# Score products of both head halves issued as one piece, in the four quarters of TensorE's array

## The chip, the cores and the metric

One core of one Trainium2 chip runs the kernel. The metric is the time of one execution on the device, in microseconds (us). The runs of the kernel before are given as a median of three; one further execution was profiled, and every row below comes from it.

## The reference, cut to what matters

128 images of 64x64 pixels and 128 channels go through a tower: a depthwise 3x3 convolution with 8x8 average pooling makes 64 tokens per image; then come a single-head attention, a mixture of ten experts (two shared, eight routed with the top two chosen), a second attention with eight heads, and a last two-layer block over channels. The change touches the scores of the second attention. Per image and head they are

```python
comp_scores = jnp.einsum('bhqd,bhkd->bhqk', q, k_c) / scale
comp_scores = jnp.where(causal_c[None, None], comp_scores, -jnp.inf)
win_scores = jnp.einsum('bhqd,bhkd->bhqk', q, k) / scale
win_scores = jnp.where(win_mask[None, None], win_scores, -jnp.inf)
all_scores = jnp.concatenate([comp_scores.astype(f32), win_scores.astype(f32), sink.astype(f32)], axis=-1)
attn = jax.nn.softmax(all_scores, axis=-1).astype(x.dtype)
```

With 64 tokens there are 64 window keys, 15 compressed keys (together LK = 79) and one sink column, so 80 scores per query and head. The head dimension is 16.

## The kernel before, in words

The images are worked on in 16 groups of eight (512 tokens, four tiles of 128 tokens, two images per tile). Four stages lie one iteration apart: while group g is tokenised (tok), group g-1 is in its first attention (att), g-2 in the experts (ffn) and g-3 in the second attention and last block (sec); 19 iterations in all. In the text "group n" is the n-th group (from 0) whose second attention is in the stretch looked at.

The order of work is written out by hand. ORDER (from line 57) holds one list of pieces per engine for one iteration, and each engine works through its own list strictly in order; semaphores make the pieces wait for each other. Nothing is planned at run time. The names of the pieces that matter here:

- score (PE line 637, DVE line 1271): the scores of one tile and one half of the heads. There are eight per group, n = 0 to 7, tile n // 2, half n % 2. TensorE first writes the mask and sink of 4 heads x 80 columns into the half's own PSUM bank (L647: place_b times limit_b, bf16, all 128 output partitions), and then adds two products (L651, fp32, 316 columns), one per image of the tile. A product contracts over the 64 partitions of the half (rows 0 to 63 or 64 to 127 of the array) and has 64 output partitions (columns 0 to 63 or 64 to 127). Each fp32 product stands in the trace as two matmul records, its two passes. From n = 2 on the mask waits until VectorE has read piece n - 2, that is the last piece in the same bank.
- VectorE reads a score piece with a maximum (L1275) and a subtraction into e3 (L1277), in its own list's order, with other work between some pieces.
- exp (ACT, L904): two exponentials of 1280 columns, behind pieces 3 and 7. In ScalarE's list the piece stands ahead of narrow.5's copy.
- turn and value (L662, L671): the transposes of e3 and the products with the values. turn.0 needs both exponentials. They use the same two banks, sec_bank[0] and sec_bank[1].
- post.0 and post.1 (L418, L681): the output projection; VectorE adds its result at L1293, and the last block follows.
- lift, widen, narrow (L566, L581 to L583, L593 and L597): the routed experts' blocks, 15 per group. widen.7 uses the bank of narrow.5, so it waits until ScalarE has copied narrow.5's result.
- pool.u.k (L446, L450, L456): pooling products. pool.1.3 waits for VectorE's inner.1.1 (L1064), which stands behind score.1 in VectorE's list. att.7 and att.8 (L418, L489) are the transposes and products of the first attention.

Each of these has its own wait, for example for the score pieces

```python
if n >= 2:
    eng.wait_ge(s3_step, at(s3_step, g, 2 * (n - 2) + 2))
```

where s3_step counts two steps of VectorE per piece.

Of the kernel before, what the change touches and what calls it, by code (L numbers as in the profile page):

```python
# [19 lines left out]
NI, HW, C = 128, 64, 128  # L20
P = 128
BX = 8
L = BX * BX
# [11 lines left out]
LK = L + LC  # L35
LCP = 16
HH = HEADS // 2
# [25 lines left out]
        up.0 up.1 table up.2 down.0 up.3 down.1 down.2 up.4 up.5 out' up.6 down.3 down.4 up.7 down.5 down.6  # L63
        down.7 lift.0 pool.0.0 pool.0.1 widen.0 lift.1 widen.1 att.1 lift.2 narrow.0 lift.3 pool.0.2 att.2 lift.4
        widen.2 att.3 pre.2 narrow.1 pre.3 pool.0.3 widen.3 pre.4 att.4 pre.6 lift.5 narrow.2 pool.1.0 pool.1.1
        lift.6 narrow.3 pre.5 widen.4 pre.7 pool.1.2 widen.5 score.0 lift.7 score.1 score.2 pool.1.3 narrow.4
        score.3 lift.8 score.4 score.5 att.7 score.6 score.7 narrow.5 widen.6 att.8 turn.0 widen.7 pool.2.0
        lift.9 pool.2.1 turn.1 value.0 narrow.6 lift.10 turn.2 pool.2.2 value.1 widen.8 turn.3 pool.2.3 value.2
        narrow.7 turn.4 value.3 lift.11 att.10 turn.5 value.4 widen.9 att.11 value.5 turn.6 narrow.8 turn.7
        value.6 widen.10 att.12 lift.12 value.7 narrow.9 narrow.10 lift.13 post.0 widen.11 post.1 widen.12  # L70
        lift.14 narrow.11 pool.3.0 widen.13 narrow.12 pool.3.1 widen.14 narrow.13 pool.3.2 post.3 narrow.14
        pool.3.3 post.4 post.5""",
    act="""
        hidden.0 table hidden.1 hidden.2 hidden.3 hidden.4 hidden.5 out' hidden.6 hidden.7 lift.0 pool.0.0 lift.1
        widen.0 lift.2 att.1 narrow.0 lift.3 widen.1 att.2 pre.2 narrow.1 att.3 lift.4 gate widen.2 pool.0.2
# [16 lines left out]
    pool="""  # L92
# [23 lines left out]
def program(nc, x, conv_w, conv_b, wq, bq, wk, bk, gate_w, gate_b, w1, b1, w2, bias, sb2,  # L116
            swq, swqs, swk, swks, swv, swkc, swvc, swo, comp_gate, sink, tw1, tb1, tw2, tb2,
            ident_c, block_c, cos_c, sin_c, mask1_c, limit_c, place_c, part_c, heads_c, before_c, route_c, out):
    with ExitStack() as ctx:
# [16 lines left out]
        def at(s, g, k):  # L136

            return g * per[id(s)] + k
# [275 lines left out]
        def _(eng):  # L414
# [186 lines left out]
            def layer2(g, b, kind, n=0):  # L601
# [21 lines left out]
                elif kind == "pre" and n in (6, 7):  # L623
                    if n == 6:
                        eng.wait_ge(rope_read, at(rope_read, g, 4))
                        for t in range(T):
                            mm = nc.tensor.matmul(b1[:, t * C:(t + 1) * C], x3t[:, t * P:(t + 1) * P], second["v"][:],
                                                  start=True, stop=True)
                    else:
                        eng.wait_ge(xc_step, at(xc_step, g, 8))  # L630
                        eng.wait_ge(kc_ready, at(kc_ready, g, 1))
                        for k in range(2):
                            mm = nc.tensor.matmul(b0[:, k * C:(k + 1) * C],
                                                  xc[:, 4 * k:4 * k + 4, :].rearrange("p i w -> p (i w)"), second["vc"][:],
                                                  start=True, stop=True)
                    mm.then_inc(v_done, 1)
                elif kind == "score":
                    t, half = n // 2, n % 2
                    bank = sec_bank[half]
                    if n == 0:  # L640
                        eng.wait_ge(keys_ready, at(keys_ready, g, 1))
                        eng.wait_ge(kc_ready, at(kc_ready, g, 1))
                        eng.wait_ge(v_ready, at(v_ready, g, 2))
                    if n >= 2:
                        eng.wait_ge(s3_step, at(s3_step, g, 2 * (n - 2) + 2))
                    wide, rows = bank[:, 0:HH * (LK + 1)], slice(half * C // 2, (half + 1) * C // 2)
                    nc.tensor.matmul(wide, place_b[:], limit_b[:, half].rearrange("p h k -> p (h k)"),  # L647
                                     start=True, stop=False)
                    for im in range(2):
                        tok = (2 * t + im) * L  # L650
                        mm = nc.tensor.matmul(  # L651
                            wide[im * L:(im + 1) * L].rearrange("p (h k) -> p h k", h=HH)[:, :, 0:LK],
                            q3[rows, tok:tok + L], keys_h[rows, :, 2 * t + im, :],
                            start=False, stop=True)
                    mm.then_inc(scored, 1)
                elif kind == "turn":
                    if n == 0:
                        eng.wait_ge(e3_ready, at(e3_ready, g, 2))
                    if n >= 1:
                        eng.wait_ge(p3t_ready, at(p3t_ready, g, n))  # L660
                    for h in range(HH):
                        mm = nc.tensor.transpose(b0[0:LK + 1, h * P:(h + 1) * P], e3[:, n, h, :], ident[:])  # L662
                    mm.then_inc(p3_turned, 1)
                elif kind == "value":
                    t, half = n // 2, n % 2
                    eng.wait_ge(p3t_ready, at(p3t_ready, g, n + 1))
                    if n >= 1:
                        eng.wait_ge(o3_ready, at(o3_ready, g, n))
                    for h in range(HH):
                        for im in range(2):  # L670
                            mm = nc.tensor.matmul(b1[im * L:(im + 1) * L, h * (HD + 1):(h + 1) * (HD + 1)],  # L671
                                                  p3t[:, half, h, im * L:(im + 1) * L],
                                                  values[:, 2 * t + im, half * HH + h, :], start=True, stop=True)
                    mm.then_inc(o3_done, 1)
                elif kind == "post" and n == 0:
                    eng.wait_ge(o3_ready, at(o3_ready, g, 8))
                    turn_tiles(b0, lambda t: o3[:, t, :], ident[:]).then_inc(o3_turned, 1)
                elif kind == "post" and n == 1:
                    eng.wait_ge(o3t_ready, at(o3t_ready, g, 1))
                    for t in range(T):  # L680
                        mm = nc.tensor.matmul(b1[:, t * P:(t + 1) * P], o3t[:, t * P:(t + 1) * P], second["o"][:],  # L681
                                              start=True, stop=True)
                    mm.then_inc(wo_done, 1)
                elif kind == "post" and n == 3:
                    eng.wait_ge(x4_ready, at(x4_ready, g, 4))
                    turn_tiles(b0, lambda t: x3[:, t, :], ident[:]).then_inc(x4_turned, 1)
                elif kind == "post" and n == 4:
                    eng.wait_ge(x4t_ready, at(x4t_ready, g, 1))
                    nc.tensor.matmul(b1[:], tw1_s[:], x3t[:], start=True, stop=True).then_inc(up_done, 1)
                elif kind == "post" and n == 5:  # L690
                    eng.wait_ge(up_ready, at(up_ready, g, 1))
                    for t in range(T):
                        mm = nc.tensor.matmul(b0[:, t * P:(t + 1) * P], o3t[:, t * P:(t + 1) * P], tw2_s[:],
                                              start=True, stop=True)
                    mm.then_inc(mlp_done, 1)
# [797 lines left out]
```

## Time and profile before

| | us |
|---|---|
| runs of the kernel before, median of 3 | 1969.28 |
| lowest and highest of them | 1950.7 and 1969.51 |
| the profiled execution's own time | 1981.56 |
| span of the profiled execution (first to last instruction) | 1979.8 |
| TensorE busy in it | 1588.2 |
| VectorE busy in it | 1417.9 |
| mean granted clock of TensorE | 0.866 |

The span is what the views of the trace cover; the time of the execution lies 1.8 us above it. A granted clock of 1.00 is 2.4 GHz, 0.50 is 1.2 GHz, and a value between them is a mean over a stretch that has both. Start times count from the start of the span. PE is TensorE, DVE is VectorE, ACT is ScalarE and POOL is GpSimd.

### The profile page before, as it was taken

The numbers are of one execution on the slowest core, as the hardware profiler recorded it, in microseconds if no ns is written. First come the engines' busy times: TensorE is split into PE (matmuls) and PEld (weight loads), VectorE is DVE, ScalarE is ACT, GpSimd is POOL, SyncE is SP. The second block draws the span as 40 slices with busy tenths as digits, with TensorE's granted clock in tenths as the row PEclk, the third lists the DMA queues.
The fourth block names the chain that finished last, engine by engine and source line by source line (L and its number), as shares of the span: only waits on it lengthen the run. The fifth ranks groups of instructions, "written<-read, shape, count | busy, mean of one in ns | idle before, by whom it ended". The sixth has DMA issues, their size and how long they took to land.

```text
span 1979.8 us, 42922 instructions
## 1 busy us (share of the span) xinstructions
PE 1588.2 (80%) x14896; PEld 1190.4 (60%) x14896; DVE 1417.9 (72%) x3372; ACT 1002.2 (51%) x2581; POOL 797.3 (40%) x643
## 2 busy tenths in 40 slices
PE   0132878989898988989898989898898989998846
PEld 0021665757666675767576676667676766666623
DVE  3767677878877787888778788778887787642322
ACT  0112546555555646565555547365656555564622
POOL 2335363544526263545436263625444352504020
PEclk9975888998879797998889789879989897979965
DMA  7556564453735544554536455445546364202000
GB/s 295 216 192 230 195 221 181 162 208 145 260 134 193 211 170 163 196 202 155 211 143 227 172 188 220 143 178 201 205 141 231 140 240 156 62 7 62 13 22 6
DMA packets 109125, 331.56 MB, mean 167 GB/s; under 512 B 13662, under 2 KB 87585, under 8 KB 92412
## 3 DMA queue, kind: packets, MB, share of 16 engines
q1 hardware_dynamic: 86416, 300.90, 41.3%
q0 software_dynamic: 8992, 19.42, 2.9%
q10 hardware_dynamic: 13516, 8.50, 1.4%
q8 instruction: 133, 2.18, 0.5%
q14 instruction: 68, 0.56, 0.1%
HBM read 299.48 MB, written 29.29 MB: 166 GB/s over the span
## 4 chain that ended last, share of the span: by engine, by line
PE 43%; DVE 18%; POOL 15%; issue 11%; DMA 6%; ACT 5%; ACTq 2%; SPq 0%; POOLq 0%; DVEq 0%
PE hid_bank L597 10%; PE sec_bank L651 5%; POOL yg L1375 5%; POOL xbuf L1364 4%; DMA xbuf<-in_x 4%; PE hid_bank L582 3%; PE sec_bank L671 3%; PE sec_bank L662 3%; PE hid_bank L581 3%; DVE xbuf L1064 3%; DVE xbuf L1060 3%; POOL rows_d L1353 2%; DVE xc L1269 2%; POOL rs L1336 2%; PE hid_bank L583 2%
## 5 line engine op out<-in xcount | busy, mean ns | idle before, releaser
L1364 POOL TENSOR_TENSOR xbuf<-xbuf 128x512 f32<-128x512 f32 x256 | 343.3, 1341 | 587.3 <-DVE xbuf L1060 578.7
L597 PE MATMUL hid_bank<-w_s,hid 128*128 x1920 | 329.5, 324 | 0.0
L842 ACT ACTIVATE hid<-hid_bank,bias_t 128x128 f32<-128x128 f32 x960 | 272.1, 377 | 83.2 <-PE hid_bank L583 78.9
L597 PEld LDWEIGHTS hid_bank<-w_s,hid 128*128 128x128 f32 x1920 | 278.4, 223 | 18.7
L581 PE MATMUL hid_bank<-xt,w_b 128*128 128x128 bf16 x960 | 221.1, 239 | 57.8 <-ACT ys L852 30.3
L1060 DVE TENSOR_TENSOR xbuf<-xbuf 128x1536 f32<-128x1536 f32 x128 | 224.3, 1752 | 19.8 <-DMA xbuf<-in_x 19.8
L1353 POOL DMA_INDIRECT rows_d<-x2r,spot_i x128 | 159.5, 1246 | 195.8 <-DVE owned L1211 163.4
L582 PE MATMUL hid_bank<-xt,w_b 128*128 128x128 bf16 x960 | 222.2, 240 | 0.4
L583 PE MATMUL hid_bank<-xt,w_b 128*128 128x128 bf16 x960 | 218.4, 236 | 0.0
L1085 DVE SCALAR_TENSOR_TENSOR taps<-pooled_s,tapw,taps 128x256 f32<-128x256 f32 (+1 forms) x416 | 208.6, 501 | 8.3
L1068 DVE TENSOR_TENSOR xbuf<-xbuf 128x1024 bf16<-128x1024 f32 x128 | 173.5, 1355 | 24.2 <-DMA xbuf<-in_x 24.2
L833 ACT ACTIVATE xt<-down_bank 128x256 bf16<-128x256 bf16 x240 | 93.2, 388 | 185.6 <-PE down_bank L566 185.5
L1375 POOL DMA_INDIRECT yg<-outs_d,spot_i x128 | 145.4, 1136 | 54.0 <-issue 39.5
L581 PEld LDWEIGHTS hid_bank<-xt,w_b 128*128 x960 | 98.8, 103 | 86.7 <-issue 78.4
L825 ACT ACTIVATE hid<-hid_bank,b_s 128x512 f32<-128x512 f32 x128 | 87.3, 687 | 120.8 <-PE hid_bank L530 98.2
L769 ACT ACTIVATE pooled_s<-pool_bank 128x384 f32<-128x384 f32 x192 | 95.0, 497 | 89.2 <-PE pool_bank L450 70.9
L1275 DVE TENSOR_REDUCE m<-sec_bank 128x4 f32<-128x320 f32 x128 | 62.7, 490 | 106.0 <-PE sec_bank L651 105.4
L1064 DVE TENSOR_TENSOR xbuf<-xbuf 128x512 bf16<-128x512 f32 x128 | 107.5, 840 | 43.2 <-POOL xbuf L1364 43.1
L446 PE MATMUL pool_bank<-block_b,xbuf 128*128 128x48 bf16 x1024 | 49.7, 190 | 106.7 <-DVE xbuf L1064 62.7
L909 ACT ACTIVATE p3t<-sec_bank 80x512 f32<-80x512 f32 x128 | 76.3, 596 | 116.3 <-PE sec_bank L662 116.3
L542 PEld LDWEIGHTS down_bank<-w_s,hid 128*128 128x128 f32 x1024 | 129.1, 198 | 10.1 <-issue 1.1
L1336 POOL TENSOR_TENSOR rs<-ve,power 128x4 f32<-128x4 f32 x64 | 83.9, 1310 | 124.6 <-DVE ve L1045 123.0
(216 smaller groups left out, 3344.2 us busy)
## 6 DMA issues: line engine op xcount, KB each, us to landing
xbuf<-in_x SPq DMA_DIRECT2D x128, 2048.0 KB
rows_s<-rows_d SPq DMA_DIRECT2D x48, 320.0 KB, 8.1
outs_d<-ys SPq DMA_DIRECT2D x240, 64.0 KB, 1.8
out<-h ACTq DMA_DIRECT2D x16, 256.0 KB
w_s<-in_w ACTq DMA_DIRECT2D x1, 2560.0 KB
hid<-in_w POOLq DMA_DIRECT2D x10, 256.0 KB, 3.4
rows_d<-x2r,spot_i POOLq DMA_INDIRECT x128
yg<-outs_d,spot_i POOLq DMA_INDIRECT x128
```

The costliest lines, as they stand in the source:

```text
L581: nc.tensor.matmul(out_q, w_high, high, start=True, stop=False)
L582: nc.tensor.matmul(out_q, w_low, high, start=False, stop=False)
L583: mm = nc.tensor.matmul(out_q, w_high, low, start=False, stop=True)
L597: mm = nc.tensor.matmul(hid_bank[n % 2][:, 0:P], hid[:, n % RING, q * P:(q + 1) * P], w_q, start=False, stop=q == FC - 1)
L842: ins = nc.scalar.activation(hid[:, n % RING, cols], hid_bank[n % 2][:, cols], ACT.Gelu, bias=bias_t[:, q, j:j + 1])
L1060: nc.vector.tensor_tensor(v[:, :, 1:6:2, :], v[:, :, 1:6:2, :], v[:, :, 2:7:2, :], ALU.add) \
L1064: nc.vector.tensor_tensor(halves[k][:, :, 1, 0, :], blocks[k][:, :, 1, :], halves[k][:, :, 1, 1, :], ALU.subtract).then_inc(inner_low, 1)
L1068: nc.vector.tensor_tensor(halves[k][:, :, 0:8:7, 0, :], blocks[k][:, :, 0:8:7, :], halves[k][:, :, 0:8:7, 1, :], ALU.subtract).then_inc(en ...
L1085: nc.vector.scalar_tensor_tensor(dst, src, w, dst, ALU.mult, ALU.add).then_inc(tapped, 1)
L1353: nc.gpsimd.indirect_dma_start(out=rows_d, out_offset=bass.IndirectOffsetOnAxis(spot_i[b][:, k:k + 1], 0), in_=x2r[b][:, k % T, :], in_off ...
L1364: nc.gpsimd.tensor_tensor(v[:, :, 1, :], v[:, :, 1, :], v[:, :, 2 * k + 3, :], ALU.add) \
L1375: nc.gpsimd.indirect_dma_start(out=yg[:, n, :], out_offset=None, in_=outs_d, in_offset=bass.IndirectOffsetOnAxis(spot_i[b][:, n:n + 1], 0)) \
```

## The change

A score piece now covers one tile with both halves of the heads, so there are four per group (n is the tile). TensorE writes the two masks, one in each bank, and then issues four products, alternating between the halves, for the first image and then for the second. The mask of each half waits until VectorE has read the same half of the tile before. The semaphore scored still counts once per half, and the lists of VectorE and ScalarE are unchanged: VectorE still reads eight pieces. In TensorE's list the eight score pieces become four: old 0 and 1 stand behind lift.7, which moves ahead of them; old 2 and 3 stand behind narrow.4; old 4 and 5 behind lift.8; old 6 and 7 behind att.7.

```diff
--- before.py
+++ after.py
@@ -63,13 +63,12 @@
         up.0 up.1 table up.2 down.0 up.3 down.1 down.2 up.4 up.5 out' up.6 down.3 down.4 up.7 down.5 down.6
         down.7 lift.0 pool.0.0 pool.0.1 widen.0 lift.1 widen.1 att.1 lift.2 narrow.0 lift.3 pool.0.2 att.2 lift.4
         widen.2 att.3 pre.2 narrow.1 pre.3 pool.0.3 widen.3 pre.4 att.4 pre.6 lift.5 narrow.2 pool.1.0 pool.1.1
-        lift.6 narrow.3 pre.5 widen.4 pre.7 pool.1.2 widen.5 score.0 lift.7 score.1 score.2 pool.1.3 narrow.4
-        score.3 lift.8 score.4 score.5 att.7 score.6 score.7 narrow.5 widen.6 att.8 turn.0 widen.7 pool.2.0
-        lift.9 pool.2.1 turn.1 value.0 narrow.6 lift.10 turn.2 pool.2.2 value.1 widen.8 turn.3 pool.2.3 value.2
-        narrow.7 turn.4 value.3 lift.11 att.10 turn.5 value.4 widen.9 att.11 value.5 turn.6 narrow.8 turn.7
-        value.6 widen.10 att.12 lift.12 value.7 narrow.9 narrow.10 lift.13 post.0 widen.11 post.1 widen.12
-        lift.14 narrow.11 pool.3.0 widen.13 narrow.12 pool.3.1 widen.14 narrow.13 pool.3.2 post.3 narrow.14
-        pool.3.3 post.4 post.5""",
+        lift.6 narrow.3 pre.5 widen.4 pre.7 pool.1.2 widen.5 lift.7 score.0 pool.1.3 narrow.4 score.1 lift.8
+        score.2 att.7 score.3 narrow.5 widen.6 att.8 turn.0 widen.7 pool.2.0 lift.9 pool.2.1 turn.1 value.0
+        narrow.6 lift.10 turn.2 pool.2.2 value.1 widen.8 turn.3 pool.2.3 value.2 narrow.7 turn.4 value.3 lift.11
+        att.10 turn.5 value.4 widen.9 att.11 value.5 turn.6 narrow.8 turn.7 value.6 widen.10 att.12 lift.12
+        value.7 narrow.9 narrow.10 lift.13 post.0 widen.11 post.1 widen.12 lift.14 narrow.11 pool.3.0 widen.13
+        narrow.12 pool.3.1 widen.14 narrow.13 pool.3.2 post.3 narrow.14 pool.3.3 post.4 post.5""",
     act="""
         hidden.0 table hidden.1 hidden.2 hidden.3 hidden.4 hidden.5 out' hidden.6 hidden.7 lift.0 pool.0.0 lift.1
         widen.0 lift.2 att.1 narrow.0 lift.3 widen.1 att.2 pre.2 narrow.1 att.3 lift.4 gate widen.2 pool.0.2
@@ -635,24 +634,26 @@
                                                   start=True, stop=True)
                     mm.then_inc(v_done, 1)
                 elif kind == "score":
-                    t, half = n // 2, n % 2
-                    bank = sec_bank[half]
+                    t = n
                     if n == 0:
                         eng.wait_ge(keys_ready, at(keys_ready, g, 1))
                         eng.wait_ge(kc_ready, at(kc_ready, g, 1))
                         eng.wait_ge(v_ready, at(v_ready, g, 2))
-                    if n >= 2:
-                        eng.wait_ge(s3_step, at(s3_step, g, 2 * (n - 2) + 2))
-                    wide, rows = bank[:, 0:HH * (LK + 1)], slice(half * C // 2, (half + 1) * C // 2)
-                    nc.tensor.matmul(wide, place_b[:], limit_b[:, half].rearrange("p h k -> p (h k)"),
-                                     start=True, stop=False)
+                    for half in range(2):
+                        if n >= 1:
+                            eng.wait_ge(s3_step, at(s3_step, g, 2 * (2 * n - 2 + half) + 2))
+                        nc.tensor.matmul(sec_bank[half][:, 0:HH * (LK + 1)], place_b[:],
+                                         limit_b[:, half].rearrange("p h k -> p (h k)"), start=True, stop=False)
                     for im in range(2):
                         tok = (2 * t + im) * L
-                        mm = nc.tensor.matmul(
-                            wide[im * L:(im + 1) * L].rearrange("p (h k) -> p h k", h=HH)[:, :, 0:LK],
-                            q3[rows, tok:tok + L], keys_h[rows, :, 2 * t + im, :],
-                            start=False, stop=True)
-                    mm.then_inc(scored, 1)
+                        for half in range(2):
+                            rows = slice(half * C // 2, (half + 1) * C // 2)
+                            wide = sec_bank[half][im * L:(im + 1) * L, 0:HH * (LK + 1)]
+                            mm = nc.tensor.matmul(wide.rearrange("p (h k) -> p h k", h=HH)[:, :, 0:LK],
+                                                  q3[rows, tok:tok + L], keys_h[rows, :, 2 * t + im, :],
+                                                  start=False, stop=True)
+                            if im == 1:
+                                mm.then_inc(scored, 1)
                 elif kind == "turn":
                     if n == 0:
                         eng.wait_ge(e3_ready, at(e3_ready, g, 2))
```

## Rows read from the trace of the kernel before

**Rows 1.** engines and shares of the chain, from the page (numbers 1 and 4)

```profile
PE 1588.2 (80%) x14896; PEld 1190.4 (60%) x14896; DVE 1417.9 (72%) x3372; ACT 1002.2 (51%) x2581; POOL 797.3 (40%) x643
...
PE 43%; DVE 18%; POOL 15%; issue 11%; DMA 6%; ACT 5%; ACTq 2%; SPq 0%; POOLq 0%; DVEq 0%
```

**Rows 2.** groups by line, shapes apart: busy us, mean ns, idle before, releaser

```profile
L651 PE MATMUL sec_bank<-keys_h,q 64*64 64x316 f32 x512 | 131.8, 601 | 0.0
...
L1275 DVE TENSOR_REDUCE m<-sec_bank 128x4 f32<-128x320 f32 x128 | 62.7, 490 | 106.0 <-PE sec_bank L651 105.4
```

**Rows 3.** stretches score.0 to narrow.5: length; busy of PE, PEld, DVE, ACT, POOL; clock

```profile
439.77:450.57 10.80, 9.96 (x74) 4.29 (x74) 9.32 (x19) 8.20 (x24) 3.57 (x3) 1.00 0.51 193
545.08:561.01 15.93, 15.24 (x73) 6.28 (x74) 9.83 (x19) 8.45 (x24) 3.02 (x3) 0.59 0.35 133
```

**Rows 4.** the same view, whole periods

```profile
439.77:545.08 105.31, 96.28 (x931) 74.48 (x932) 85.44 (x207) 61.80 (x160) 50.20 (x40) 0.89 0.53 192
545.08:656.29 111.21, 99.02 (x932) 74.76 (x932) 86.78 (x207) 61.72 (x160) 49.50 (x40) 0.87 0.50 182
...
1423.07:1527.41 104.34, 93.92 (x931) 72.02 (x932) 85.33 (x207) 61.67 (x160) 49.69 (x40) 0.92 0.53 194
1527.41:1637.20 109.79, 97.86 (x931) 73.79 (x932) 88.80 (x207) 61.67 (x160) 49.13 (x40) 0.87 0.51 184
```

**Rows 5.** timeline of group 1: start, duration, engine, line, operands [idle before, releaser]

```profile
439.77 0.30 PE L647 MATMUL sec_bank<-limit_b,place_b 67*128 67x320 bf16 x1 [0.25 <-ACT values L896]
...
440.00 0.76 PE L651 MATMUL sec_bank<-keys_h,q 64*64 64x316 f32 x4
...
440.69 0.28 PE L566 MATMUL down_bank<-ident_b,rows_s 128*128 128x128 bf16 x2
...
440.79 0.49 DVE L1275 TENSOR_REDUCE m<-sec_bank 128x4 f32<-128x320 f32 x1 [2.08 <-PE sec_bank L651]
...
441.32 0.49 DVE L1277 TENSOR_TENSOR e<-sec_bank,m 128x320 f32<-128x320 f32 x1
...
443.54 0.37 PE L446 MATMUL pool_bank<-block_b,xbuf 128*128 128x48 bf16 x8 [0.69 <-DVE xbuf L1064]
...
445.20 0.30 PE L647 MATMUL sec_bank<-limit_b,place_b 67*128 67x320 bf16 x1
...
450.57 0.23 PE L593 MATMUL hid_bank<-bias_b,owned 24*128 24x128 bf16 x1
...
451.77 1.27 ACT L904 ACTIVATE e<-e 128x1280 f32<-128x1280 f32 x1 [1.08 <-DVE e L1277]
...
453.33 0.60 PE L662 MATMUL sec_bank<-ident,e 128*80 128x128 f32 x4
```

**Rows 6.** chain that ended last, in order of time, VectorE's step behind post.1 of group 1

```profile
485.33 0.70 DVE h L1293
```

**Rows 7.** timeline of group 2, clock at 1.2 GHz

```profile
551.69 0.47 PE L647 MATMUL sec_bank<-limit_b,place_b 67*128 67x320 bf16 x1
...
552.10 1.32 PE L651 MATMUL sec_bank<-keys_h,q 64*64 64x316 f32 x4
...
553.35 0.40 PE L566 MATMUL down_bank<-ident_b,rows_s 128*128 128x128 bf16 x2
...
561.01 0.28 PE L593 MATMUL hid_bank<-bias_b,owned 24*128 24x128 bf16 x1
...
562.18 1.27 ACT L904 ACTIVATE e<-e 128x1280 f32<-128x1280 f32 x1 [2.45 <-DVE e L1277]
...
565.64 0.60 PE L662 MATMUL sec_bank<-ident,e 128*80 128x128 f32 x4
```

**Rows 8.** stretches ahead of a fall of the clock, columns as in rows 3

```profile
536.15:541.15 5.00, 2.88 (x41) 2.29 (x41) 4.75 (x11) 4.57 (x12) 0.00 (x0) 1.00 0.79 272
541.15:544.56 3.41, 3.41 (x34) 3.22 (x33) 2.34 (x3) 1.91 (x8) 1.51 (x2) 0.50 0.76 327
545.08:547.97 2.89, 2.82 (x17) 0.91 (x17) 1.77 (x4) 1.65 (x7) 0.50 (x1) 1.00 0.00 0
```


## The prediction

> **What bounds the kernel now.** I read the page's engine and chain lines first [rows 1]. TensorE is busy 80% of the 1979.8 us span and has the largest share of the chain that ended last, 43%; VectorE has 18% and GpSimd 15%. No engine is alone: a delay counts if it reaches the chain. The groups by line [rows 2] price the part under change: 512 records of the score products (L651, two passes for each of 256 products), 601 ns each in the mean, and 128 maxima on VectorE (L1275, 0.49 us). The reader should see that the products end 105.4 us of VectorE's idle time.
>
> The stretches from score.0 to narrow.5 [rows 3] show TensorE's clock. In group 1 the stretch takes 10.80 us at a granted 1.00; in group 2 it takes 15.93 us at 0.59. Of the 16 groups, 5 (1, 5, 8, 10, 14) look like the first and 11 like the second, or stand at 0.50 throughout; rows 3 are the first of each sort. A whole period, score.0 to the next score.0 [rows 4], follows it: of the four periods in mid-run that hold a full-clock stretch the first and last take 105.31 and 104.34 us (mean of the four 105.78), of seven with the low clock 111.21 and 109.79 (mean 110.61). The difference is 4.83 us.
>
> Next the timeline of group 1, at 2.4 GHz [rows 5]. Mask at 439.77, products at 440.00, next instruction (lift.7) at 440.69: a piece holds TensorE for 0.92 us, its products for 0.69. The four records of a piece (two images, two passes) end 0.76 us after the first starts, though one takes 0.60 us in the mean of the group: **the two image quarters of one piece already overlap.** What doesn't is one half of the heads with the other. VectorE starts its maximum 0.03 us after the products' end and is through with the subtraction at 441.81, 1.02 us later. So the engines are nearly in balance, 0.92 against 1.02 us, because the two banks let TensorE write one while VectorE reads the other. turn.0 starts at 453.33, behind att.8 and only 0.29 us behind the end of the second exponential (453.04). The chain [rows 6] runs over TensorE through these pieces and the turns and values to post.1, whose result VectorE adds at 485.33; the last scatters, the gathers and the next group's sums hang behind that. So what delays turn.0 delays the period.
>
> For most of group 2's stretch the clock is 1.2 GHz [rows 7]: a piece takes 1.66 us with 0.41 from mask to product, its products 1.25, longer than VectorE's 1.02. TensorE binds there. The second exponential ends at 563.45 and turn.0 comes at 565.64, so 2.2 us are to spare.
>
> **The change, part by part.** (a) Products. All four quarters of a pair are issued in a row; if the row halves overlap as the column halves do, a pair's products take 0.69 us for 1.38 (1.25 for 2.50 at half clock). The trace never shows two row halves at once: the bounds are these two, and I take the overlap, since the nearest rows are 64x64 tiles too and these two go to different banks. (b) Masks. The second follows the first in the same shape. No row shows that distance: it lies between 320 columns at 2.4 GHz, 0.13 us, and the 0.23 from mask to product; I take 0.13 (half clock 0.27). The change of shape is then paid once per pair: 0.13+0.23+0.69 = 1.05 us of TensorE for 1.84, saving 0.79; at half clock 0.27+0.40+1.25 = 1.92 for 3.3, saving 1.4. Over four pairs 3.2 or 5.5 us per group. (c) Waits. The products of a pair stand behind both masks, and the second mask waits until VectorE has read the second half of the pair before. The banks no longer alternate: VectorE idles while TensorE writes a pair, TensorE while VectorE reads it. Queued behind the waiting mask are att.7, narrow.5, widen.6, att.8 and turn.0, and behind them ScalarE's copies. (d) Order. Old score.2, which filled TensorE ahead of pool.1.3, goes behind narrow.4 with its partner; lift.7 goes ahead of score.0 (0.12 us). The lists of the other engines, the DMA queues' too, stay, and nothing is moved past them.
>
> The Trainium skill speaks against the change: "TensorEngine Tiling (Array Packing)", Performance Considerations, says that tiling speeds up the array but not the emptying of PSUM, which may become the bottleneck. VectorE's 1.02 us a piece [rows 5] agrees; the sums below stand without the rule.
>
> Replay at full clock, from group 1. lift.7, masks at 439.89 and 440.03, products 440.26 to 441.02, 0.26 later than now. VectorE reads from 441.05 to 443.1, then makes its two x operations, so pool.1.3 starts at 443.80 (now 443.54) and narrow.4 ends at 445.46 (now 445.20): TensorE is idle for 2.8 us ahead of pool.1.3 instead of 0.69. score.1: products 445.83 to 446.59; VectorE reads until 448.67 (it now begins that piece earlier, since it was written long before). score.2: second mask at 448.7, products 448.95 to 449.71, read, with one tap of 0.4 between, until 452.15; att.7 hides in this. score.3: products 452.43 to 453.19, read until 455.2. narrow.5 starts at 453.12 instead of 450.57, **2.55 us later**; the exponential runs from 455.25 to 456.5, and turn.0 starts at 456.6 instead of 453.33, **3.3 us later**: the saved 3.2 us of TensorE turn into waiting. ScalarE's list has the exponential ahead of narrow.5's copy, so widen.7, behind turn.0, is no earlier.
>
> Replay at half clock, from group 2. score.1: masks 551.95 and 552.22, products 552.62 to 553.94, read until 556.03. score.2: products 556.48 to 557.80, read until 560.27. score.3: products 560.70 to 562.02. narrow.5 at 561.95 instead of 561.01, 0.95 us later; VectorE is through at 564.1, the exponential at 565.4, and turn.0 (566.6) is still set by TensorE's own list. **Cost 0.95.**
>
> **Which clock.** In 536.15 to 541.15 TensorE was busy for 2.88 of 5.00 us at full clock, and just after it the clock fell [rows 8]. Three score pieces with little idle time (2.82 of 2.89 us) stood ahead of a fall as well. In the replay TensorE is idle 2.8 us ahead of pool.1.3 and about 1 us in each of two later waits. I take it that all five full-clock stretches fall to half: each costs its period's 4.83 plus 0.95, so 5 x 5.78 = 28.9; the eleven others 11 x 0.95 = 10.5; 39.4 us in all. The profiled execution would go from 1981.56 to 2021. It lies 0.6% over the median of the runs, 1969.28; on that the forecast is **1969.3 + 39.4 = 2009 us**.
>
> The Trainium skill, "TensorE: Matmul & The Clock Gate", Why this matters for your kernels, says that idle gaps between bursts of matmuls bring the throughput down. By that rule the price is the 39 of the forecast, without it the 27 of the first rival; the row of 536.15 agrees, the one of 545.08 doesn't need a gap.
>
> **Rivals.** (1) The clock keeps its present pattern: 5 x 3.3 + 11 x 0.95 = 27 us, 1996. For it: group 1 already stands 0.69 us idle ahead of pool.1.3 and keeps its clock. Against: the idle time grows fourfold. (2) The delay of half-clock groups is absorbed behind turn.0; the full-clock ones pay, 5 x 3.3 = 16 us, 1986. Against: the chain shows TensorE nearly without a break up to post.1. (3) **Not slower: denser products hold the clock at 2.4 GHz through score.** Place: the pieces ahead of pool.1.3, where group 2's clock fell from a busy stretch. Each of the 11 low groups gains 4.83 and pays 3.3, the five pay 3.3: -16.8 + 16.5, nothing, 1969. It decides from the point where 3.3/4.83 = 0.68 of the groups are rid of a low stretch, which 11 of 16 just reach; if low stretches elsewhere go too, it is faster. Against: the idle time of the replay. (4) The row halves don't overlap: 1.25 us more a pair at half clock, 16 x 4 x 1.25 = 80 on top of 39, 2089.
>
> **How the numbers follow.** Chances: forecast 0.43, (1) 0.25, (2) 0.10, (3) 0.15, (4) 0.07. The range leaves out (4) and a part of (3) and (1), and above the forecast it allows for a low stretch longer by a few us in some groups: 1963 to 2038. A measurement of this kernel tells about 1% from no change. Faster by over 1%: 0.08 (half of 3). Within 1%: 0.20 (the rest of 3, most of 2, a little of 1). Slower: 0.72.
>
> **What would show it.** Right: the four first passes of a pair start together, a pair's products hold TensorE for 0.7 us; VectorE waits before every first half and never before the second; TensorE is idle almost 3 us ahead of pool.1.3; the clock is low in nearly all score stretches. Wrong: products of a pair at 1.3 us or more (rival 4); stretches at 1.00 in most groups (rival 3); periods as before though narrow.5 is late (rival 2).

## The result and the profile after

The changed kernel takes 1999.49 us (median of 4, 1994.99 to 2001.97) against 1969.39 us of the kernel before (median of 4, 1950.7 to 1989.49). The ratio is 1.0147, with a 95% interval from 1.0108 to 1.0187: slower, by 21 to 37 us. An execution over 1.5% above the fastest of its kernel is left out of the ratios and intervals of this document, but not of its medians. The forecast was 2009 us, the range 1963 to 2038. The execution profiled after took 2000.55 us, 19 us more than the one profiled before; that earlier one lies 12 us over its median, so the medians tell the size of the change and the profiles tell its place.

The page first, engines and shares of the chain (beside [rows 1]):

```profile
PE 1543.6 (77%) x14864; PEld 1181.6 (59%) x14896; DVE 1415.3 (71%) x3372; ACT 1002.9 (50%) x2581; POOL 795.2 (40%) x643
...
PE 38%; DVE 22%; POOL 17%; issue 11%; ACT 5%; DMA 5%; ACTq 2%; POOLq 0%; SPq 0%; DVEq 0%
```

TensorE has less work, 1543.6 us for 1588.2, and a smaller share of the chain, 38% for 43%. VectorE went from 18% to 22% of the chain with the same work. The groups by line, shapes apart (beside [rows 2]):

```profile
L652 PE MATMUL sec_bank<-keys_h,q 64*64 64x316 f32 x512 | 75.0, 671 | 0.0
...
L1276 DVE TENSOR_REDUCE m<-sec_bank 128x4 f32<-128x320 f32 x128 | 62.3, 486 | 144.8 <-PE sec_bank L652 144.8
...
L645 PE MATMUL sec_bank<-limit_b,place_b 67*128 67x320 bf16 x128 | 47.1, 410 | 43.7 <-DVE e L1278 38.2 <-ACT values L897 3.9
```

The products' busy time fell from 131.8 to 75.0 us. The reader should see the other two groups: VectorE's idle time behind the products grew from 105.4 to 144.8 us, and the masks now stand 38.2 us behind VectorE's subtraction. Each engine waits for the other.

Stretches of the changed kernel: score.0's first mask to narrow.5 in groups 1 and 2, then whole periods of groups 1, 2 and 11. The columns are those of [rows 3]: stretch, length, busy time of PE, PEld, DVE, ACT and POOL, granted clock, DMA share, GB/s.

```profile
436.78:452.31 15.53, 10.72 (x71) 4.44 (x72) 8.65 (x17) 8.36 (x24) 3.56 (x3) 0.67 0.36 135
544.85:561.27 16.42, 11.60 (x72) 5.23 (x72) 8.66 (x17) 8.32 (x24) 3.71 (x3) 0.59 0.34 132
436.78:544.85 108.07, 91.53 (x930) 70.07 (x933) 88.19 (x207) 61.78 (x161) 48.81 (x40) 0.91 0.51 187
544.85:658.82 113.97, 97.77 (x929) 75.73 (x932) 86.96 (x207) 61.66 (x160) 49.40 (x40) 0.84 0.49 178
1542.07:1654.28 112.21, 98.69 (x929) 76.64 (x932) 85.43 (x207) 61.90 (x161) 49.87 (x40) 0.82 0.49 180
```

Group 1 took 10.80 us at 1.00 before [rows 3]; now it takes 15.53 at 0.67. Counted from the first mask to turn.0, as below too, none of the groups 1 to 11 has a full-clock score stretch (a granted clock of 0.95 or more) any more: they stand at 0.58 to 0.66, and there were four. From the first mask of group 1 (436.78) to that of group 12 (1654.28) it is eleven periods of 110.68 us in the mean; before it was (1637.20 - 439.77) / 11 = 108.86, with 105.78 in the four full-clock periods and 110.61 in the seven others [rows 4].

Timeline of group 2 (start, duration, engine, line, operands, idle time before and its releaser), beside [rows 7]:

```profile
544.85 0.43 PE L645 MATMUL sec_bank<-limit_b,place_b 67*128 67x320 bf16 x2 [0.18 <-ACT values L897]
...
545.21 0.77 PE L652 MATMUL sec_bank<-keys_h,q 64*64 64x316 f32 x8
546.02 0.49 DVE L1276 TENSOR_REDUCE m<-sec_bank 128x4 f32<-128x320 f32 x1 [2.08 <-PE sec_bank L652]
...
548.65 0.50 PE L445 MATMUL pool_bank<-block_b,xbuf 128*128 128x48 bf16 x8 [2.67 <-DVE xbuf L1065]
...
551.49 0.74 PE L645 MATMUL sec_bank<-limit_b,place_b 67*128 67x320 bf16 x2
...
552.16 1.33 PE L652 MATMUL sec_bank<-keys_h,q 64*64 64x316 f32 x8
...
553.54 0.49 DVE L1276 TENSOR_REDUCE m<-sec_bank 128x4 f32<-128x320 f32 x1 [3.30 <-PE sec_bank L652]
...
554.07 0.49 DVE L1278 TENSOR_TENSOR e<-sec_bank,m 128x320 f32<-128x320 f32 x1
...
554.47 0.48 DVE L1276 TENSOR_REDUCE m<-sec_bank 128x4 f32<-128x320 f32 x1
...
554.62 0.45 PE L645 MATMUL sec_bank<-limit_b,place_b 67*128 67x320 bf16 x1 [0.80 <-DVE e L1278]
554.99 0.49 DVE L1278 TENSOR_TENSOR e<-sec_bank,m 128x320 f32<-128x320 f32 x1
...
555.54 0.45 PE L645 MATMUL sec_bank<-limit_b,place_b 67*128 67x320 bf16 x1 [0.48 <-DVE e L1278]
...
555.92 1.33 PE L652 MATMUL sec_bank<-keys_h,q 64*64 64x316 f32 x8
...
557.30 0.49 DVE L1276 TENSOR_REDUCE m<-sec_bank 128x4 f32<-128x320 f32 x1 [1.73 <-PE sec_bank L652]
...
561.26 0.28 PE L592 MATMUL hid_bank<-bias_b,owned 24*128 24x128 bf16 x1
...
563.35 1.27 ACT L905 ACTIVATE e<-e 128x1280 f32<-128x1280 f32 x1 [3.27 <-DVE e L1278]
...
565.66 0.60 PE L663 MATMUL sec_bank<-ident,e 128*80 128x128 f32 x4
```

Four things are to be seen. The eight records of a pair end 0.77 us after the first starts (545.21), as the four of one half did: all four quarters overlap. TensorE then stands idle for 2.67 us ahead of pool.1.3. VectorE waits before every first half (3.30 and 1.73 us here) and not before the second (554.47). And the second mask waits for VectorE (0.48 us) after the first mask waited too (0.80).

### The profile page after: what moved, and what is told of

The parts are those of the page before. It is cut to its first block, busy times and chain, and to the rows that moved or that the text cites. A ratio compares the mean times of both kernels' runs of the same rounds, so it can differ in the third digit from the quotient of the medians.

```text
span 1998.7 us, 42890 instructions
## 1 busy us (share of the span) xinstructions
PE 1543.6 (77%) x14864; PEld 1181.6 (59%) x14896; DVE 1415.3 (71%) x3372; ACT 1002.9 (50%) x2581; POOL 795.2 (40%) x643
## 4 chain that ended last, share of the span: by engine, by line
PE 38%; DVE 22%; POOL 17%; issue 11%; ACT 5%; DMA 5%; ACTq 2%; POOLq 0%; SPq 0%; DVEq 0%
PE hid_bank L596 9%; POOL yg L1376 6%; POOL xbuf L1365 4%; POOL rows_d L1354 4%; PE sec_bank L652 4%; DMA xbuf<-in_x 3%; PE hid_bank L581 3%; PE sec_bank L663 3%; PE sec_bank L672 3%; PE hid_bank L580 3%; DVE xbuf L1061 3%; DVE xbuf L1065 3%; DVE e L1278 2%; DVE m L1276 2%; DVE xc L1270 2%
## 5 line engine op out<-in xcount | busy, mean ns | idle before, releaser
L580 PE MATMUL hid_bank<-xt,w_b 128*128 128x128 bf16 x960 | 225.0, 244 | 57.0 <-ACT ys L853 30.9
L581 PE MATMUL hid_bank<-xt,w_b 128*128 128x128 bf16 x960 | 225.8, 244 | 0.5
L582 PE MATMUL hid_bank<-xt,w_b 128*128 128x128 bf16 x960 | 222.1, 240 | 0.0
L1276 DVE TENSOR_REDUCE m<-sec_bank 128x4 f32<-128x320 f32 x128 | 62.3, 486 | 144.8 <-PE sec_bank L652 144.8
L445 PE MATMUL pool_bank<-block_b,xbuf 128*128 128x48 bf16 x1024 | 49.7, 190 | 131.7 <-DVE xbuf L1065 88.0
L445 PEld LDWEIGHTS pool_bank<-block_b,xbuf 128*128 128x128 bf16 x1024 | 42.7, 101 | 153.0 <-issue 72.7
```

Source lines behind the costliest of these rows:

```text
L580: nc.tensor.matmul(out_q, w_high, high, start=True, stop=False)
L581: nc.tensor.matmul(out_q, w_low, high, start=False, stop=False)
L582: mm = nc.tensor.matmul(out_q, w_high, low, start=False, stop=True)
```

## The experiments

Unless a group is named, a period below is the mean over groups 1 to 11 of one profile, from the first mask of group 1 to that of group 12. Ratios are to runs of the kernel before in the same set. Beside e1 to e4 it took 1970.0 us, beside e5 to e7 1970.4, beside e8 and e9 2048.4, beside e10 and e11 2020.9. The changed kernel itself was not run beside any of them. The first and the last of these four sets have the same chip number on record, so the level isn't the chip's alone. Across sets only ratios can be compared.

**e1: the changed list with the old pieces.** Undoes the joint piece and keeps the order.

```diff
-        ... widen.5 score.0 lift.7 score.1 score.2 pool.1.3 narrow.4 score.3 lift.8 score.4 score.5 att.7 score.6
-        score.7 ...
+        ... widen.5 lift.7 score.0 score.1 pool.1.3 narrow.4 score.2 score.3 lift.8 score.4 score.5 att.7 score.6
+        score.7 ...
```

> The eight score pieces of the kernel before, one half each, in the places of the changed TensorE list (old score.2 behind narrow.4, lift.7 ahead of score.0); no joint piece, no joint waits. If the cost of the change lies in the joint piece (both masks and both waits ahead of all four products), this run is close to the kernel before, 0.99 to 1.00 of it. If the loss of cover ahead of pool.1.3 is what costs, then TensorE idles about 2 us there, the clock falls in nearly all score stretches, and one more piece of 1.65 us stands behind narrow.4: 5 x (4.83 + 1.65) + 11 x 1.65 = 50 us slower than before, that is more than the 30 us of the changed kernel, since the products aren't packed.

Measured: 2011.16 us, ratio 1.0205 (1.0177 to 1.0232), period 111.43 us. Two of its stretches, from the first mask to narrow.5:

```profile
554.14:571.58 17.44, 15.69 (x71) 6.32 (x71) 9.83 (x19) 8.45 (x24) 3.02 (x3) 0.59 0.32 121
1446.28:1462.61 16.33, 14.59 (x73) 5.28 (x72) 9.82 (x19) 8.46 (x24) 3.78 (x3) 0.66 0.34 128
```

So the order alone, with one piece less ahead of pool.1.3, costs 41 us, more than the whole change with its 30. The joint piece is not what makes it slow: in this list it gives back about 11 us by the ratios, though the two intervals overlap a little. The clock is low in all the mid-run stretches, as expected; TensorE is idle for 1.75 us ahead of pool.1.3, and the expected loss was 50 us.

**e2: the changed kernel with score.1 ahead of pool.1.3.**

```diff
-        lift.6 narrow.3 pre.5 widen.4 pre.7 pool.1.2 widen.5 lift.7 score.0 pool.1.3 narrow.4 score.1 lift.8
+        lift.6 narrow.3 pre.5 widen.4 pre.7 pool.1.2 widen.5 lift.7 score.0 score.1 pool.1.3 narrow.4 lift.8
```

> The changed kernel with its score.1 moved from behind narrow.4 to ahead of pool.1.3. Theory (joint waits cost only where nothing covers them; the wait ahead of pool.1.3 is the largest): turn.0 comes 2.3 us earlier than before in a stretch at half clock and 2.1 us later in one at full clock; with the clock low everywhere 5 x (4.83 - 2.3) - 11 x 2.3 = 13 us faster than the kernel before, some 1957 us. Rival (the packed products as such, or the waits between VectorE and TensorE in score.2 and score.3, make the loss): this stays near the changed kernel, within 5 us of 1999.

Measured: 1957.87 us, ratio 0.9947 (0.9907 to 0.9986), period 107.05. The stretch to narrow.5 and the period of group 2:

```profile
545.50:558.65 13.15, 10.05 (x71) 4.91 (x72) 8.56 (x17) 8.33 (x24) 3.73 (x3) 0.72 0.42 161
545.50:654.59 109.09, 95.27 (x929) 74.98 (x932) 85.08 (x207) 61.89 (x161) 51.16 (x40) 0.86 0.51 185
```

13.15 us to narrow.5 instead of 16.42. One piece moved by two places turns 30 us of loss into 12 of gain (between 3 and 18 by the interval); the expectation was 13. Its condition, the clock low everywhere, didn't hold: e2's stretches stand at 0.70 to 0.89, and what of the 12 us is the clock's isn't separated.

**e5: old pieces in e2's order.**

```diff
-        ... score.0 lift.7 score.1 score.2 pool.1.3 narrow.4 score.3 lift.8 score.4 score.5 att.7 score.6 ...
+        ... lift.7 score.0 score.1 score.2 score.3 pool.1.3 narrow.4 lift.8 score.4 score.5 att.7 score.6 ...
```

> The eight pieces of the kernel before in the places of e2's list: old score.0 to score.3 ahead of pool.1.3, the rest behind narrow.4 and lift.8. Beside e2 it tells what the joint piece does with the order the same. Replay: at full clock narrow.5 0.1 us and turn.0 0.25 us later than in the kernel before (e2: 2.1 us later), at half clock 0.95 us earlier (e2: 2.3 us earlier). With all stretches at half clock 5 x 3.9 - 11 x 0.95 = 9 us slower than before, with the clocks of before 9 us faster. Theory (packing gains at half clock, loses at full): e5 is slower than e2 by 5 to 20 us as long as the stretches are mostly at half clock. Rival (the order makes e2's whole gain): e5 is as fast as e2 or faster.

Measured: 1958.57 us, ratio 0.9945 (0.9909 to 0.9981). The theory asked for 5 to 20 us more than e2; there is no difference. Two stretches show why:

```profile
544.39:554.91 10.52, 9.96 (x72) 4.33 (x72) 9.17 (x19) 8.33 (x24) 3.71 (x3) 1.00 0.48 179
751.20:766.11 14.91, 14.73 (x73) 6.22 (x72) 9.65 (x19) 8.45 (x24) 3.09 (x3) 0.61 0.37 142
```

Five of its eleven mid-run stretches stand at full clock and take 10.5 us, the others are long. e2 has none at 0.95 or more up to turn.0 (two up to narrow.5), but its low ones are shorter. These look like two effects of opposite sign and the same size. With the order put right no worth of the joint piece can be told, within the 0.4% that either interval reaches to each side; that is what the rival of the expectation said.

**e3: e2, with other work of VectorE between the pairs, and narrow.5 between score.2 and score.3.**

```diff
-        score.2 att.7 score.3 narrow.5 widen.6
+        score.2 att.7 narrow.5 score.3 widen.6
...
-        att.7 score.4 tap.0.0 score.5 tap.0.1 score.6 score.7 inner.2.0 tap.0.2
+        att.7 tap.0.0 tap.0.1 score.4 score.5 inner.2.0 tap.0.2 score.6 score.7
```

> As e2, and VectorE's list spread so that other work stands between the pairs (tap.0.0 and tap.0.1 between the second and third pair, inner.2.0 and tap.0.2 between the third and fourth), and narrow.5 between TensorE's score.2 and score.3. Theory of the joint waits: the waits are covered, VectorE's idle time ahead of its maxima falls by 1 us and more a group, turn.0 is 0.2 us earlier than in e2, so 3 us to 8 us below e2. Rival (TensorE's clock and nothing else sets the stretch): equal to e2 within 2 us.

Measured: 1954.14 us, ratio 0.9873 (0.9812 to 0.9935), against e2's 0.9947. VectorE's idle time behind the products fell from 100.8 to 66.7 us, 2 us a group. The medians are 4 us apart, in the range expected, the ratios 15 us: one of e3's four executions took 1932.57 us and pulls its ratio down, which by the medians alone is 0.992. The intervals overlap, so the step from e2 to e3 isn't settled.

**e4: the changed kernel, its idle time ahead of pool.1.3 filled.** The list has "score.0 fill pool.1.3". The filler products write into the bank that narrow.4 writes next; they change no result.

```diff
+                elif kind == "fill":
+                    n = NS * FC + 4
+                    eng.wait_ge(hid_made, at(hid_made, g, n + 1))
+                    for _ in range(8):
+                        nc.tensor.matmul(hid_bank[n % 2][:], w1_b[:, 0, 0, 0:P], w1_b[:, 0, 0, :],
+                                         start=True, stop=True)
```

> The changed kernel with eight bf16 products of 128x512 on constant weights, written over by narrow.4 later, in the idle time ahead of pool.1.3 (1.7 us at full clock, 3.4 at half). They add nothing to the output. Theory (the idle time ahead of pool.1.3 brings the clock down): the granted clock of the score stretches rises to 0.9 or 1.00 in most groups and a stretch from the first mask to narrow.5 takes 13.4 us instead of 16.4; a period falls by 1.5 to 2 us, 20 to 30 us in all, to 1975. Rival (the score products with a part of the array, or something earlier, bring it down): the clock of the stretches stays at 0.6 and the run is the same or some us slower.

Measured: 1981.95 us, ratio 1.0057 (1.0029 to 1.0086), period 108.82. The stretches to narrow.5 of groups 2 and 8:

```profile
547.45:561.54 14.09, 10.70 (x78) 4.60 (x80) 8.65 (x17) 8.33 (x24) 3.73 (x3) 0.82 0.40 150
1199.04:1212.79 13.75, 10.37 (x79) 4.60 (x80) 8.65 (x17) 8.33 (x24) 2.99 (x3) 0.84 0.41 153
```

Work that computes nothing takes 18 us off, where 20 to 30 were expected. The clock up to narrow.5 rose to 0.82 and 0.84, not to the 0.9 or 1.00 expected: it now falls later, 8.7 to 11.9 us behind the first mask in the groups that come with 2.4 GHz.

**e6: e4, and the first mask of score.2 and score.3 written six times while the second waits.**

```diff
+                        more = 5 if n >= 2 and half == 0 else 0
+                        for r in range(more + 1):
+                            nc.tensor.matmul(sec_bank[half][:, 0:HH * (LK + 1)], place_b[:],
+                                             limit_b[:, half].rearrange("p h k -> p (h k)"), start=True, stop=r < more)
```

> As e4, and in score.2 and score.3 the first mask is written six times over while the second mask waits (the same values, nothing in the output changes). Theory (idle time brings the clock down, the joint waits then cost what the replay at full clock says): the score stretches stand at 0.95 or more, narrow.5 starts 13.3 us and turn.0 16.8 us behind the first mask, periods of 108.5 to 109 us, the whole near e4 or 5 us below it. Rival (the clock of this stretch does not depend on how busy it is): as e4, clock 0.73 to 0.82 and narrow.5 at 13.7 to 14.3 us.

Measured: 1956.37 us, ratio 0.9929 (0.9895 to 0.9962), period 106.63. Stretch to narrow.5 and period of group 5, then its timeline:

```profile
862.62:875.58 12.96, 10.26 (x89) 5.01 (x90) 8.65 (x17) 8.34 (x24) 3.59 (x3) 1.00 0.43 163
862.62:971.36 108.74, 91.92 (x946) 71.31 (x950) 86.55 (x207) 61.67 (x160) 48.49 (x40) 0.94 0.51 186
```

```profile
862.62 0.43 PE L647 MATMUL sec_bank<-limit_b,place_b 67*128 67x320 bf16 x2
...
864.21 1.67 PE L713 MATMUL hid_bank<-w_b 128*128 128x512 bf16 x7 [0.45 <-ACT hid L851]
...
866.43 0.37 PE L445 MATMUL pool_bank<-block_b,xbuf 128*128 128x48 bf16 x8 [0.55 <-DVE xbuf L1073]
...
875.58 0.23 PE L592 MATMUL hid_bank<-bias_b,owned 24*128 24x128 bf16 x1
...
877.68 1.27 ACT L913 ACTIVATE e<-e 128x1280 f32<-128x1280 f32 x1 [3.02 <-DVE e L1286]
...
879.00 0.64 PE L665 MATMUL sec_bank<-ident,e 128*80 128x128 f32 x4 [0.49 <-ACT e L913]
```

Ten of the eleven stretches are at full clock. This is the changed kernel as the replay at full clock had it: narrow.5 12.96 us behind the first mask and turn.0 16.38, where the kernel before has 10.80 and 13.56 [rows 5]; the two masks' own shift by lift.7 is 0.12 more. turn.0 follows the exponential, 0.05 us behind its end (878.95). So at full clock the joint waits do put turn.0 off by 2.9 us. In the period less of it is seen: e6's ten full-clock periods are 106.43 us in the mean (group 5's 108.74 is the longest), 0.65 more than the four of the kernel before. The fillers change the clock in the rest of the period too, so what the waits alone cost there isn't shown. The expectations of 108.5 to 109 us a period and of a time at most 5 us below e4 were missed: e6 is 25 us faster than e4 by the ratios.

**e7: the kernel before, with three filler products in its own gap ahead of pool.1.3.** The edit is e4's, on the kernel before, with three products instead of eight and "fill" ahead of pool.1.3 in its list.

> The kernel before with three bf16 products of 128x512 on constant weights (0.65 us at full clock) in its own 0.69 us gap ahead of pool.1.3; they add nothing to the output. Theory (idle time in this stretch is what brings the clock down): most of its 11 low stretches stand at 1.00, each worth up to 4.83 us, 20 to 50 us faster than before. Rival (its score products with two quarters of the array bring it down, with a gap or without): 10 or 11 stretches stay low and the time is that of before, within 5 us.

Measured: 1924.71 us, ratio 0.9772 (0.968 to 0.9865), period 105.12. Timeline of group 1, then its stretch, a low one (group 5), and a whole period:

```profile
428.55 0.30 PE L647 MATMUL sec_bank<-limit_b,place_b 67*128 67x320 bf16 x1 [0.25 <-ACT values L902]
...
431.80 0.59 PE L710 MATMUL hid_bank<-w_b 128*128 128x512 bf16 x2 [0.16 <-issue]
...
432.34 0.37 PE L446 MATMUL pool_bank<-block_b,xbuf 128*128 128x48 bf16 x8
```

```profile
428.55:439.36 10.81, 10.51 (x75) 4.49 (x77) 9.33 (x19) 8.19 (x24) 3.59 (x3) 1.00 0.51 194
847.73:864.70 16.97, 16.57 (x76) 6.79 (x77) 9.82 (x19) 8.45 (x24) 2.97 (x3) 0.57 0.33 125
428.55:534.18 105.63, 94.62 (x931) 72.63 (x935) 87.35 (x207) 61.54 (x160) 50.02 (x40) 0.92 0.53 192
```

Where [rows 5] has 0.69 us idle ahead of L446, the fillers (L710) stand. Eight of the eleven mid-run stretches are at full clock instead of four. The lowest ratio of the study is that of the kernel before with 0.6 us of useless work a group. How so short a filler does it is open. In group 2 of the kernel before the clock falls at 547.97 [rows 8], while L446 there starts at 548.86 behind 0.62 us of idle time, so this fall comes ahead of the gap that the fillers fill.

**e8 and e9: both kinds of pieces with the clock held.** e8 is e3 with three fillers ahead of score.1 and the first mask written four times; e9 is e5 with three fillers ahead of its score.3.

> e3 (joint pieces, waits covered by a spread list) with three filler products ahead of its score.1 and the first mask of score.2 and score.3 written four times, so that the clock has less idle time to fall on. In e3 the periods with a full-clock score stretch took 102.3 to 108.5 us. Theory (clock and waits are the two costs): nearly all stretches at 0.95 or more, turn.0 at 15.0 us behind the first mask, 15 to 30 us below e3, 1925 to 1940. Rival (packing helps most where the clock is low, so at full clock nothing is left of it): slower than e9 by 10 us or more.

> e5 (one-half pieces, the same four ahead of pool.1.3) with three filler products in the wait ahead of its score.3. Theory: nearly all stretches at 1.00, narrow.5 at 10.6 us and turn.0 at 13.3 us behind the first mask as in e5's full-clock groups, 20 to 35 us below e5, 1925 to 1940. Beside e8 it shows whether the joint piece is worth anything once the clock is held: its turn.0 should be 1.7 us earlier than e8's.

Measured, where the kernel before takes 2048.4 us: e8 2015.78 us, ratio 0.9847 (0.98 to 0.9893); e9 2016.49, ratio 0.9876 (0.9801 to 0.9951). All of e8's stretches are full, and turn.0 comes 15.0 us behind the first mask. This one is group 1's, from the first mask to turn.0:

```profile
435.50:450.50 15.00, 12.07 (x109) 7.04 (x110) 13.37 (x25) 9.66 (x26) 2.96 (x3) 1.00 0.38 143
```

The 15 to 30 us expected below e3 didn't come, though: the ratios are 0.9847 and 0.9873. Of e9's eleven stretches only four are full, and e5 had five without fillers; here the expectation failed. Nine of e9's eleven groups come to their first mask with 1.2 GHz in the 5 us ahead of it, so the run says little about the fillers' place. The comparison of the pieces stays open with it, and two kernels were run again.

**e10 and e11: e7 and e8 again, on one chip.**

> e7 once more (the kernel before with three filler products), on the same chip and against the same runs of before as e11. If e7's gain is one of the kernel and not of its chip: ratio to before 0.97 to 0.985.

> e8 once more (joint pieces, spread list, clock held by fillers). Both kernels then have nearly all score stretches at full clock; e7's turn.0 comes 13.6 us behind the first mask and e8's 15.0. If the joint piece costs its waits at full clock even with a spread list, e11 is slower than e10 by 5 to 20 us; if VectorE's work moved into the stretch pays that back later in the period, the two are equal within 5 us.

Measured: e10 1988.86 us, ratio 0.9865 (0.9821 to 0.991); e11 1983.17, ratio 0.9822 (0.9778 to 0.9866). Both beat both kernels of the case. The intervals overlap: with the clock held and the list spread, joint pieces are as good as alternating ones, and no better that could be told. e7's gain came out smaller this time, 1.35% for 2.3%, just outside the 1.5 to 3% expected; its two intervals overlap.

## Why the prediction was right

**The products.** Right: four quarters overlap, 0.77 us a pair, so rival (4) fell. The second mask came 0.13 us behind the first (two masks end 0.43 us after the first starts, one takes 0.30), the value taken.

**The waits.** Right in place and nearly in size. 2.8 us idle ahead of pool.1.3 were forecast, 2.67 measured. At full clock narrow.5 was to be 2.55 us late and turn.0 3.3; e6, in which the changed list runs at full clock, has 2.16 and 2.82, with lift.7's 0.12 us 2.3 and 2.9. The term that was a little off is VectorE's: 2.05 us were taken for reading a pair, twice the 1.02 of a piece and a pause, and it takes 1.94 (553.54 to 555.48), because the second maximum (554.47) starts ahead of the end of the first subtraction's record. Over four pairs that is the 0.4 us.

**The clock.** Right, and the largest term: the five full-clock stretches were to fall, at 4.83 us each, 24.2 us. In the profile after, no mid-run stretch is full, nor is group 14's (0.71), and the periods are as long as the low ones were, 110.68 for 110.61. What takes the clock down was argued from one row. The stretches ahead of and behind the first mask tell more (columns as in [rows 3]; group 1 and 2 of the kernel before, then group 1 of the changed one):

```profile
434.77:439.77 5.00, 3.65 (x39) 2.79 (x39) 3.93 (x4) 3.80 (x12) 1.49 (x2) 1.00 0.87 367
540.08:545.08 5.00, 4.36 (x38) 3.81 (x39) 3.41 (x3) 3.25 (x12) 2.03 (x2) 0.66 0.74 318
```

```profile
431.78:436.78 5.00, 3.77 (x40) 2.89 (x41) 3.92 (x4) 3.88 (x13) 1.50 (x2) 1.00 0.88 370
436.78:441.90 5.12, 2.45 (x32) 1.52 (x33) 3.87 (x6) 5.09 (x16) 1.03 (x1) 1.00 0.00 0
441.90:455.56 13.66, 11.52 (x61) 5.99 (x60) 7.84 (x19) 4.42 (x10) 2.53 (x2) 0.50 0.41 155
```

In the kernel before, four of the groups 1 to 11 come with 2.4 GHz in all of the 5 us ahead of the first mask, and all four keep it up to turn.0; seven come like group 2, and none does. In the changed kernel five come with 2.4 GHz and all five lose it, as do all seven such groups of e1, whose gap ahead of pool.1.3 is 1.75 us; in e6 all six keep it. So the gaps, and what stands in them, decide for such groups: e4 and e6 add nothing but work in idle time, and are worth 18 and 43 us by the ratios. Idle time as a sum is not the measure: up to narrow.5 e6 has 2.7 us of it at 1.00 (12.96 - 10.26), e5's low stretch 0.2 (14.91 - 14.73). And a rival is left: the fillers are also products over the whole array, where the scores' are 64x64 tiles, and no run fills the gap with anything else. The Trainium skill's rule ("TensorE: Matmul & The Clock Gate", Why this matters for your kernels: idle gaps between bursts of matmuls bring the throughput down) points the same way, but it means longer gaps than these; the measured 2.67 and 1.75 us decide.

**The half-clock price.** Mis-sized. 0.95 us for each of 16 groups was 15.2 of the 39.4 us. In group 2 narrow.5 is 16.42 us behind the first mask instead of 15.93, and turn.0 20.81 (565.66 - 544.85) instead of 20.56, to which lift.7's 0.12 comes: 0.6 and 0.4 us late. Of that nothing is seen in the period (0.07). Without the term the forecast would be 24 us.

**The size.** Partly luck. Between the two profiled executions the eleven periods grew by 20.1 us (1217.5 for 1197.4), which is the four falls of the clock (4 x 4.83 = 19.3) and hardly more, and the whole by 19; the forecast of 39.4 was made for that execution, at 1981.56 us. The medians are 30 us apart because the execution profiled before lies 12 us above its median. For these other 11 us no trace stands.

**Rival (2).** It said that the half-clock delay is absorbed behind turn.0, and was right about this part, but it priced the clock's fall at nothing.

**The cause in fewer words than the forecast had.** It laid the cost at the joint waits and the lost alternation. e1 and e2 show that the list has more of it: the same order without joint waits is 41 us slower than the kernel before, the joint piece with its cover back is 12 us faster. The joint waits put turn.0 off by 2.9 us only at full clock, which the changed list doesn't have. Rival (3), denser products that hold the clock, is refuted in this list: the clock fell in every mid-run stretch. Rival (1) fell with it.

**Where TensorE's saved time went.** 44.6 us less of busy time [rows 1]. It came back as waits of the masks (43.7 us ahead of the masks in all, where the kernel before has 5.9) and as idle time ahead of L445 (131.7 us for 106.7), and the lower clock stretched what was left.

## What to carry to other kernels

Merging two pieces makes the engine's work denser and its waits joint. Before merging two pieces that alternate between two banks, see what stands ahead of the next wait in the in-order list, and keep that cover, since here one piece moved by two places was worth some 40 us. Look at the granted clock of each repeat of the stretch before summing durations: the cost of a gap was less its length than the clock of what followed. If a short gap can't be closed, a few harmless products in it are worth a trial.

## What wasn't expected of the hardware

- Three bf16 products of 128x512 in a 0.69 us gap made the kernel before 2.3% faster (1.35% when run again); 8 of 11 mid-run stretches then stood at 2.4 GHz instead of 4.
- The same three products in e9's list, one piece later, left 4 of 11, though TensorE is idle there for no more than 0.3 to 0.5 us up to narrow.5. Whether their place or the state in which the groups arrive does this was not found out.
- What stands ahead of a stretch counts: in the kernel before all four groups that had 2.4 GHz in the 5 us ahead of the first mask kept it, and none of the seven others did.
- Products in the four 64x64 quarters, with two passes each, start within 0.02 us of each other and take as long as two did, at both clocks (0.77 and 1.33 us a pair).
- What the chip looks at when it lowers the clock was not found out; the runs show that it fell in all twelve groups that came with 2.4 GHz to a gap of 1.75 or 2.67 us, and in none of the four that came to one of 0.69.
